# A fused attention and mixture-of-experts block: the last two scatters issued together, and the mixed tiles at other places

## Chip, core and metric

The kernel runs on one core of a Trainium2 chip. The metric is the device time of one execution in microseconds (us); lower is better. The time before is 401.59 us, the median of 3 runs (400.23 to 401.62).

## What is computed

```python
x = x + tanh(g_xattn) * sparse_attention(ctx_512, layernorm(x))   # 4 x 512 x 512
xl = layernorm(x).reshape(2048, 512)                              # 2048 tokens
shared = silu(xl @ shared_gate_w) * (xl @ shared_up_w) @ shared_down_w
top_val, top_idx = top_k(xl @ router_w, 2)                        # 2 of 8 experts
xin = probs.T[:, :, None] * xl[None]                              # probs: sigmoid(top_val), else 0
gate, up = split(einsum('etd,edf->etf', xin, gate_up_w), 2)       # 512 -> 2 x 256
expert_out = einsum('eti,eid->etd', silu(gate) * up, down_w)      # 256 -> 512
return x + tanh(g_ffn) * (shared + expert_out.sum(axis=0))
```

All numbers are float32. Each token goes to two of eight experts, so there are 4096 pairs of token and expert.

## The kernel before

The first half (the attention matrix, the search for its threshold, the two norms, the router) is not touched by the change, and it is not needed to follow it. Its last results are the rows of tokens and the table of pairs, both complete at about 210 us.

**Tiles and jobs.** The pairs are packed into 34 tiles of 128 rows (`MT = 34`). 25 of them are pure: all 128 rows belong to one expert. Nine are mixed (`MIX = 9`): four groups of 32 rows, each group with its own expert. `MIXED` names the places in the order of tiles at which the mixed ones stand. Tiles and the 16 blocks of the shared expert are jobs, `JOBS[0]` to `JOBS[49]`; from tile 7 (job 23) on the job is the tile's number plus 16. Tile 32 is job 48, and tile 33 is the last, job 49.

**One tile.** GpSimd gathers its rows (`gather`), TensorE turns them (`turn_rows`) and multiplies them with the expert's gate and up weights (`up`), ScalarE takes the silu (`silu_of`), VectorE multiplies (`gate`), TensorE turns the result (`turn_h`), ScalarE copies it (`turned_h`), TensorE multiplies it with the down weights (`down`), ScalarE writes the scaled product into a y buffer (`y_of`), and GpSimd adds the rows to the output in DRAM by an indirect DMA (`scatter`). TensorE's order is `up(j)`, `turn_rows`, `down(j-1)`, `turn_h(j)`, `up(j+1)`: one tile lies in the next one's shadow. All orders are written out by hand, engine by engine, and each engine works in order.

**Scatters are chained.** Two tiles can hold the same token, and a scatter that adds reads a row and writes it back. So each scatter waits until the one before has landed:

```python
pool.wait_ge(scattered, 16 * CHAIN.index(t))
```

**Mixed tiles.** For each, VectorE copies four experts' gate and up weights (`stage_up`, four copies of 128x2048) and ScalarE four down weights (`stage_down`) into a staging buffer, which is free when the mixed tile before has used it. A mixed tile can also hold one token twice. So its finished rows in the y buffer go through one more product: `fold` multiplies them with a 128x128 matrix of zeros and ones that adds up the rows of the same token, ScalarE copies the sums back (`folded_y`), and all but one of the twins are sent to a dump row. The matrices are made once by `twin_rows` (TensorE) and `find_twins` (VectorE); `scatter_rows` makes the row numbers. TensorE issues the fold of job j in the middle of `up(j + 2)`:

```python
if c == DC // 2 and folds is not None:
    fold(folds)
```

Before, `MIXED` is 9, 11, 13, ..., 25. So the product in whose middle a fold stands is that of the next mixed tile for eight of nine folds (fold of tile 9 in `up` of tile 11, and so on); only the last, that of tile 25, stands in a pure product.

**y buffers.** `y_slot` gives job j its buffer: two in turn. `Y_FROM = 100` is behind the last job, so the rule for three buffers behind it is never used.

Of the kernel before, what the change touches and what calls it, by code (L numbers as in the profile page):

```python
# [8 lines left out]
I32 = mybir.dt.int32  # L9
# [16 lines left out]
def flamingo_gated_block(nc, x, ctx_in, g_xattn, g_ffn, wq, wk, gamma_raw, router_w, gate_up_w, down_w,  # L26
# [38 lines left out]
    MIXED = (9, 11, 13, 15, 17, 19, 21, 23, 25)  # L65


    CHAIN = (0, 1, 2, 3, 4, 5, 6, 7, 8, 9, 10, 11, 12, 13, 14, 15, 16, 17, 18, 19, 20, 21, 22, 23, 24, 25, 26, 27, 28, 29, 30, 31, 32, 33)

# [14 lines left out]
    Y_FROM = 100  # L84
# [38 lines left out]
    with ExitStack() as stack:  # L123
# [122 lines left out]
        idx_s = tmp[:, 3, 32:32 + MIX].bitcast(I32)  # L246
        etab_u = tmp[0:1, 3, 64:64 + UNITS].bitcast(I32)
# [106 lines left out]
        fold_ps = sem("fold_ps")  # L354
        folded = sem("folded")
# [129 lines left out]
        def _(pool):  # L485
# [64 lines left out]
            def scatter(t):  # L550
# [119 lines left out]
        def _(act):  # L670
# [110 lines left out]
            def y_of(j):  # L781
# [222 lines left out]
            stage_down(2, 0)  # L1004
            stage_down(2, 1)
            folded_y(27)
# [4 lines left out]
            stage_down(2, 2)  # L1011
            stage_down(2, 3)
# [4 lines left out]
            stage_down(3, 0)  # L1017
            stage_down(3, 1)
            folded_y(29)
# [4 lines left out]
            stage_down(3, 2)  # L1024
            stage_down(3, 3)
# [4 lines left out]
            stage_down(4, 0)  # L1030
            stage_down(4, 1)
# [5 lines left out]
            stage_down(4, 2)  # L1037
            stage_down(4, 3)
# [4 lines left out]
            stage_down(5, 0)  # L1043
            stage_down(5, 1)
            folded_y(33)
# [4 lines left out]
            stage_down(5, 2)  # L1050
            stage_down(5, 3)
# [4 lines left out]
            stage_down(6, 0)  # L1056
            stage_down(6, 1)
            folded_y(35)
# [4 lines left out]
            stage_down(6, 2)  # L1063
            stage_down(6, 3)
# [4 lines left out]
            stage_down(7, 0)  # L1069
            stage_down(7, 1)  # L1070
            folded_y(37)
# [4 lines left out]
            stage_down(7, 2)  # L1076
            stage_down(7, 3)
# [4 lines left out]
            stage_down(8, 0)  # L1082
            stage_down(8, 1)
            folded_y(39)
# [4 lines left out]
            stage_down(8, 2)  # L1089
            stage_down(8, 3)  # L1090
# [4 lines left out]
            folded_y(41)  # L1095
# [3 lines left out]
            turned_h(43)  # L1099
            silu_of(44)  # L1100
            turned_rows(29)
            y_of(43)
            turned_h(44)
            silu_of(45)
            turned_rows(30)
            y_of(44)
            turned_h(45)
            silu_of(46)
# [17 lines left out]
        def _(pe):  # L1126
# [120 lines left out]
            def twin_rows(k):  # L1247
# [79 lines left out]
            def down(j):  # L1327
# [16 lines left out]
                for c in range(IC):  # L1344
# [4 lines left out]
                    mm = TE.matmul(y_b[j % 2][:, :], hT[:, j % 2, c], w, start=(c == 0), stop=(c == IC - 1))  # L1349
# [231 lines left out]
            up(29, 27)  # L1581
# [3 lines left out]
            up(30)  # L1585
# [3 lines left out]
            up(31, 29)  # L1589
# [15 lines left out]
            up(35, 33)  # L1605
# [3 lines left out]
            up(36)  # L1609
# [3 lines left out]
            up(37, 35)  # L1613
# [3 lines left out]
            up(38)  # L1617
# [3 lines left out]
            up(39, 37)  # L1621
# [3 lines left out]
            up(40)  # L1625
# [3 lines left out]
            up(41, 39)  # L1629
# [3 lines left out]
            up(42)  # L1633
# [3 lines left out]
            up(43, 41)  # L1637
# [3 lines left out]
            up(44)  # L1641
# [7 lines left out]
            up(46)  # L1649
# [17 lines left out]
        def _(dve):  # L1667
# [311 lines left out]
            def read_plan(g):  # L1979
# [369 lines left out]
```

## Time and profile before

| | |
|---|---|
| median of 3 runs | 401.59 us (400.23 to 401.62) |
| the profiled execution's own time | 399.67 us |
| its span on the core | 397.9 us |
| TensorE busy | 368.6 us, 93% of the span |
| VectorE, ScalarE, GpSimd busy | 228.0, 216.8, 132.8 us |
| mean granted clock of TensorE | 0.981 |

Times in the trace count from the start of the span. A scatter shows twice: as the time that GpSimd takes to write its descriptors, and as a DMA that lands later. Busy shares are means over stages with different limits, so the rows further down are of single stages.

### The profile page before, as it was taken

To read this page: it belongs to the slowest core of one execution; us is meant where nothing else is said; L and a number is where in the kernel's file an instruction comes from. 1 tells how busy PE (TensorE), PEld (TensorE's weight loads), DVE (VectorE), ACT (ScalarE), POOL (GpSimd) and SP (SyncE) were. 2 spreads that over 40 slices of the span, in tenths; PEclk is the share of its full clock that TensorE was granted. 3 is DMA by queue.
4 is the path that set the end of the run, shared out by engine and by line. 5 is a ranking of instruction groups with operands and counts; after the bars stand their busy time and mean duration, and the time that the engine had idled before them with its cause. 6 is when DMAs were issued, how large, how long until landed. Compare 5 with 4: busy or idle time off the path is not lost.

```text
span 397.9 us, 6563 instructions
## 1 busy us (share of the span) xinstructions
PE 368.6 (93%) x2018; PEld 200.8 (50%) x2018; DVE 228.0 (57%) x819; ACT 216.8 (54%) x422; POOL 132.8 (33%) x114
## 2 busy tenths in 40 slices
PE   8859789989999999999999999999999999999950
PEld 4324478467845688558766433433443343444520
DVE  1899999999998689852737635532553350110100
ACT  3594877585762696353222476656665666432320
POOL 2201121110715332222306456543644363444231
PEclk9988999999999999999999999999999999999996
DMA  7999970184767642368323564344534453446442
GB/s 222 384 387 382 389 260 6 21 235 140 218 102 188 162 79 29 53 147 174 41 41 75 87 108 83 79 75 86 83 79 67 95 80 82 69 91 108 53 51 28
DMA packets 29353, 51.12 MB, mean 128 GB/s; under 512 B 4614, under 2 KB 7942, under 8 KB 29318
## 3 DMA queue, kind: packets, MB, share of 16 engines
q0 software_dynamic: 9920, 22.16, 33.3%
q1 hardware_dynamic: 19110, 28.40, 20.3%
q8 instruction: 17, 0.28, 0.3%
q14 instruction: 18, 0.15, 0.1%
q10 hardware_dynamic: 288, 0.13, 0.1%
HBM read 28.60 MB, written 22.09 MB: 127 GB/s over the span
## 4 chain that ended last, share of the span: by engine, by line
PE 65%; DMA 11%; DVE 9%; ACT 8%; issue 4%; SPq 1%; POOLq 0%; POOL 0%; DVEq 0%; ACTq 0%
PE gate_up L1314 14%; PE down L1349 13%; PE gate_up L1299 12%; DMA out_dram<-y_sb,idx 8%; PE gate_up L1308 8%; PE down L1340 4%; PE turned_x L1281 3%; ACT junk L690 3%; PE front L1262 2%; PE turned_h L1324 2%; DMA xs<-in_x_dram 2%; PE front L1173 1%; ACT x L727 1%; DMA out_dram<-y_sb,tmp 1%; ACT sim L685 1%
## 5 line engine op out<-in xcount | busy, mean ns | idle before, releaser
L1314 PE MATMUL gate_up<-w_gu,xT 128*128 x200 | 90.0, 594 | 0.0
L2042 DVE SCALAR_TENSOR_TENSOR h<-gate_up,p_t,silu 128x256 f32<-128x256 f32 x34 | 16.4, 483 | 113.0 <-ACT silu L761 104.0
L566 POOL DMA_INDIRECT out_dram<-y_sb,idx x25 | 42.4, 1697 | 71.5 <-DMA out_dram<-y_sb,idx 33.6
L1299 PE MATMUL gate_up<-xT,w_shgu 128*128 128x128 f32 x512 | 60.0, 276 | 1.1 <-ACT xT L738 1.1
L1299 PEld LDWEIGHTS gate_up<-xT,w_shgu 128*128 128x128 f32 x512 | 58.6, 192 | 3.6 <-issue 2.3
L545 POOL DMA_INDIRECT xg<-x_rows,idx x34 | 45.2, 1329 | 43.5 <-DMA x_rows<-payl 13.5
L790 ACT ACTIVATE y_sb<-down,gates 128x512 f32<-128x512 f32 x50 | 34.2, 687 | 46.0 <-PE down L1349 31.5
L1314 PEld LDWEIGHTS gate_up<-w_gu,xT 128*128 128x128 f32 x200 | 36.3, 190 | 37.3 <-issue 37.3
L1349 PE MATMUL down<-w_dn,hT 128*128 x100 | 47.3, 597 | 0.9 <-ACT hT L770 0.9
L2025 DVE COPY sim<-w_gu 128x2048 f32 x36 | 41.8, 1222 | 0.9 <-DVE oh_e L1990 0.5
L690 ACT ACTIVATE junk<-sim,probe 128x512 int8<-128x512 f32 x44 | 31.2, 712 | 16.6 <-DVE probe L1723 9.7
L761 ACT ACTIVATE silu<-gate_up,p_t 128x256 f32<-128x256 f32 x34 | 16.1, 473 | 44.0 <-PE gate_up L1314 31.7
L801 ACT COPY xs<-w_dn 128x1024 f32 x36 | 36.0, 1046 | 1.2 <-issue 1.1
L1308 PE MATMUL gate_up<-sim,xT 128*32 128x512 f32 x288 | 34.4, 598 | 0.0
L1349 PE MATMUL down<-w_shdn,hT 128*128 128x512 f32 x64 | 30.1, 597 | 0.0
L566 POOL DMA_INDIRECT out_dram<-y_sb,tmp x9 | 15.2, 1687 | 37.9 <-ACT y_sb L805 35.1
L528 POOL DMA_DIRECT2D out_dram<-y_sb x16 | 15.1, 987 | 32.0 <-ACT y_sb L790 32.0
L1281 PEld LDWEIGHTS turned_x<-ident,xg 128*128 128x128 f32 x136 | 15.7, 140 | 19.8 <-issue 19.8
L1349 PEld LDWEIGHTS down<-w_dn,hT 128*128 128x128 f32 x100 | 17.2, 191 | 14.4 <-issue 14.4
L779 ACT COPY xT<-turned_x 128x512 f32<-128x512 f32 x34 | 19.9, 584 | 7.4 <-PE turned_x L1281 6.6
L1281 PE MATMUL turned_x<-ident,xg 128*128 128x128 f32 x136 | 21.1, 278 | 1.2 <-ACT xT L779 0.8
L1324 PEld LDWEIGHTS turned_h<-ident,h 128*128 128x128 f32 x68 | 8.6, 141 | 18.3 <-issue 17.0
(222 smaller groups left out, 503.3 us busy)
## 6 DMA issues: line engine op xcount, KB each, us to landing
w_gu<-in_L_ffn_gate_up_w_dram SPq DMA_DIRECT2D x8, 1024.0 KB
xs<-in_x_dram SPq DMA_DIRECT2D x4, 1024.0 KB, 6.9
w_dn<-in_L_ffn_down_w_dram SPq DMA_DIRECT2D x8, 512.0 KB
out_dram<-xs SPq DMA_DIRECT2D x4, 1024.0 KB, 6.9
x_rows<-x SPq DMA_DIRECT2D x4, 1024.0 KB, 5.0
out_dram<-y_sb POOLq DMA_DIRECT2D x16, 256.0 KB, 4.5
w_gu<-in_ctx_dram SPq DMA_DIRECT2D x4, 256.0 KB, 5.4
xg<-x_rows,idx POOLq DMA_INDIRECT x34, 4.3
```

The lines of the kernel that those rows point to most:

```text
L545: G.indirect_dma_start(out=xg[:, t % XG, :], out_offset=None, in_=x2_rows[0:2 * N, :] if t < EARLY else x2_rows[:, :], in_offset=bass.Indi ...
L566: G.indirect_dma_start(out=out[0:2 * N, :] if t < EARLY else out[:, :], out_offset=bass.IndirectOffsetOnAxis(ap=rows, axis=0), in_=y_at(j) ...
L690: ins = A.activation(junk[:, i - SHARE[b]], sim[:, b, i], ACT.Sign, scale=-1.0, bias=probe[:, k, i:i + 1], accum_out=sgn[:, k, i:i + 1])
L779: A.copy(xT[:, x_slot(j)], x_b[:, :].rearrange("p (c t) -> p c t", c=DC)).then_inc(xt_done, 1)
L790: A.activation(y_at(j), y_b[j % 2][:, :], ACT.Copy, scale=gates[:, 1:2]).then_inc(y_done, 1)
L801: A.copy(unit_dn[:, g], w_dn[:, bass.ds(e * (IC * D), IC * D)]).then_inc(dn_staged, 1)
L1281: mm = TE.transpose(x_b[:, c * P:(c + 1) * P], xg[:, t % XG, c * P:(c + 1) * P], ident[:, :])
L1299: mm = TE.matmul(g_b[j % 2][:, f * P:(f + 1) * P], w_shgu[:, c, f * P:(f + 1) * P], xT[:, x_slot(j), c], start=(c == 0), stop=(c == DC - 1))
L1308: mm = TE.matmul(g_b[j % 2][at, :], xT[:, x_slot(j), c, at], unit_gu[:, r, c * F2:(c + 1) * F2], start=(c == 0), stop=(c == DC - 1))
L1314: mm = TE.matmul(g_b[j % 2][:, :], xT[:, x_slot(j), c], w_gu[:, bass.ds(experts[n] * (DC * F2) + c * F2, F2)], start=(c == 0), stop=(c == ...
L1349: mm = TE.matmul(y_b[j % 2][:, :], hT[:, j % 2, c], w, start=(c == 0), stop=(c == IC - 1))
L2025: V.tensor_copy(unit_gu[:, g], w_gu[:, bass.ds(e * (DC * F2), DC * F2)]).then_inc(gu_staged, 1)
```

## The change

Three things are changed.

1. `PAIR` is tile 32. Its scatter and that of tile 33 need no longer keep apart. Rows of tile 32 whose token tile 33 holds too are sent to the dump row (`idx_p`), and their values, copied by VectorE from the PSUM bank of tile 32's product (`raw_rows`, into `joined`), are added to tile 33's rows by one more matmul in the bank of the last down product. Its 0/1 matrix and the row numbers are made beside those of the mixed tiles. `y_of(48)` waits until `raw_rows` has read the bank. Tile 33's scatter waits for that of tile 31 only.
2. `MIXED` is 9, 12, 15, 18, 20, 22, 24, 26, 28. Staging copies, folds and gates move with it. Five folds now stand in the product of a mixed tile, and four in that of a pure one (tiles 11, 14, 17 and 30).
3. `Y_FROM = 26`: from job 26 on there are three y buffers in turn.

```diff
-    MIXED = (9, 11, 13, 15, 17, 19, 21, 23, 25)
+    MIXED = (9, 12, 15, 18, 20, 22, 24, 26, 28)
...
+    PAIR = MT - 2
...
-    Y_FROM = 100
+    Y_FROM = 26
...
+        row_p = tmp[:, 3, 112:114]
+        twin_p = tmp[:, 3, 114:115]
+        idx_p = tmp[:, 3, 116:117].bitcast(I32)
+        joined = tmp[:, 1, :]
...
+                if t == PAIR:
+                    rows = idx_p
+                    pool.wait_ge(scatter_ready, 1)
...
-                    pool.wait_ge(scattered, 16 * CHAIN.index(t))
+                    pool.wait_ge(scattered, 16 * min(CHAIN.index(t), PAIR))
...
+                if j == job_of("M", PAIR):
+                    act.wait_ge(raw_ready, 1)
                 A.activation(y_at(j), y_b[j % 2][:, :], ACT.Copy, scale=gates[:, 1:2]).then_inc(y_done, 1)
...
+                if k == 2:
+                    mm = TE.matmul(f_b[0][:, P:2 * P], row_p[:, 1:2].to_broadcast([P, P]), ident[:, :], start=True,
+                                   stop=True)
...
-                    mm = TE.matmul(y_b[j % 2][:, :], hT[:, j % 2, c], w, start=(c == 0), stop=(c == IC - 1))
+                    mm = TE.matmul(y_b[j % 2][:, :], hT[:, j % 2, c], w, start=(c == 0),
+                                   stop=(c == IC - 1 and j < NJ - 1))
+                if j == NJ - 1:
+                    pe.wait_ge(raw_ready, 1)
+                    pe.wait_ge(twins_done, 3)
+                    mm = TE.matmul(y_b[j % 2][:, :], fold_m[:, MIX * P:(MIX + 1) * P], joined, start=False, stop=True)
...
+                    V.scalar_tensor_tensor(row_p, f_b[1][:, hi - lo - 2:hi - lo], 1.0, unused[:, hi - lo - 2:hi - lo],
+                                           ALU.subtract, ALU.add)
...
+                if k == 2:
+                    both = fold_m[:, MIX * P:(MIX + 1) * P]
+                    link(V.tensor_scalar(both, f_b[0][:, P:2 * P], row_p[:, 0:1], None, ALU.is_equal))
+                    ins = V.tensor_reduce(twin_p, both, AX_X, ALU.add)
...
+                link(V.tensor_scalar(unused[:, MIX:MIX + 1], row_p[:, 0:1], dump, None, ALU.subtract))
+                link(V.tensor_tensor(unused[:, MIX:MIX + 1], unused[:, MIX:MIX + 1], twin_p, ALU.mult))
+                V.tensor_tensor(idx_p, row_p[:, 0:1], unused[:, MIX:MIX + 1], ALU.subtract).then_inc(scatter_ready, 1)
...
+            def raw_rows():
+                dve.wait_ge(y_ps, job_of("M", PAIR) + 1)
+                V.tensor_copy(joined, y_b[job_of("M", PAIR) % 2][:, :]).then_inc(raw_ready, 1)
```

**TensorE around the first fold.** The rows run from the down product of mixed tile 9 (job 25) to the middle of `up` of tile 11 (job 27). `xs` and `sim` are the staged weights of a mixed tile, `front<-y_sb,x` is the fold. Before:

```order
L1340 MATMUL down<-xs,hT 32x512 [waits dn_staged,y_done,ht_done]
L1340 MATMUL down<-xs,hT 32x512 x7
L1324 MATMUL turned_h<-ident,h 128x128 [waits ht_done,h_ready]
L1324 MATMUL turned_h<-ident,h 128x128
L1308 MATMUL gate_up<-sim,xT 32x512 [waits gu_staged,xt_done,h_ready]
L1308 MATMUL gate_up<-sim,xT 32x512 x7
L1262 MATMUL front<-y_sb,x 128x512 [waits twins_done,y_done]
L1308 MATMUL gate_up<-sim,xT 32x512 x8
```

The same place in the changed kernel:

```order
L1357 MATMUL down<-xs,hT 32x512 [waits dn_staged,y_done,ht_done]
L1357 MATMUL down<-xs,hT 32x512 x7
L1341 MATMUL turned_h<-ident,h 128x128 [waits ht_done,h_ready]
L1341 MATMUL turned_h<-ident,h 128x128
L1331 ISA [waits xt_done,h_ready]
L1331 MATMUL gate_up<-w_gu,xT 128x512
L1331 ISA
L1331 MATMUL gate_up<-w_gu,xT 128x512
L1279 MATMUL front<-y_sb,x 128x512 [waits twins_done,y_done]
L1331 ISA
L1331 MATMUL gate_up<-w_gu,xT 128x512
```

Tile 11 is pure now, so the fold stands between whole matmuls and not between those of 32 columns.

**VectorE behind the ninth twin search.** The rows are the end of `find_twins(2)` and `scatter_rows`; `stage_up(1)`, `weight_of(11)` and `gate(26)` come behind them on the same engine in both kernels. Before:

```order
L2001 TENSOR_SCALAR x<-front,tmp 128x128 [waits twin_ps]
L2002 SCALAR_TENSOR_TENSOR tmp<-front,tmp,upper 128x128
L2008 TENSOR_SCALAR unused<-tmp,cols 128x9 [waits twins_done]
L2009 TENSOR_TENSOR unused<-unused,tmp 128x9 [waits vector_step]
L2010 TENSOR_TENSOR tmp<-tmp,unused 128x9 [waits vector_step]
```

In the changed kernel:

```order
L2025 TENSOR_SCALAR x<-front,tmp 128x128 [waits twin_ps]
L2026 SCALAR_TENSOR_TENSOR tmp<-front,tmp,upper 128x128
L2030 TENSOR_SCALAR x<-front,tmp 128x128
L2031 TENSOR_REDUCE tmp<-x 128x1 [waits vector_step]
L2036 TENSOR_SCALAR unused<-tmp,cols 128x9 [waits twins_done]
L2037 TENSOR_TENSOR unused<-unused,tmp 128x9 [waits vector_step]
L2038 TENSOR_TENSOR tmp<-tmp,unused 128x9 [waits vector_step]
L2039 TENSOR_SCALAR unused<-tmp,cols 128x1
L2040 TENSOR_TENSOR unused<-unused,tmp 128x1 [waits vector_step]
L2041 TENSOR_TENSOR tmp<-tmp,unused 128x1 [waits vector_step]
```

Five instructions are added ahead of `stage_up(1)`: two at 128x128 and three at one column.

**ScalarE at the end.** The rows are `y_of(48)`, `turned_h(49)` and `y_of(49)`. Before:

```order
L790 ACTIVATE y_sb<-down,gates 128x512 [waits scattered,y_ps]
L770 COPY hT<-turned_h 128x256 [waits y_ps,ht_ps]
L790 ACTIVATE y_sb<-down,gates 128x512 [waits scattered,y_ps]
```

In the changed kernel:

```order
L804 ACTIVATE y_sb<-down,gates 128x512 [waits raw_ready,scattered,y_ps]
L782 COPY hT<-turned_h 128x256 [waits y_ps,ht_ps]
L804 ACTIVATE tmp<-down,gates 128x512 [waits scattered,y_ps]
```

The order is the same; the first has one wait more, with the other two queued behind it, and the last writes into the third y buffer.

## Rows read from the trace of the kernel before

**Rows 1.** Windows: busy time and count of each engine, PEclk, DMA share, GB/s.

```profile
200.00:231.00 31.00, 31.00 (x189) 17.28 (x189) 18.56 (x62) 11.67 (x20) 12.23 (x9) 1.00 0.43 68
...
370.00:385.00 15.00, 13.80 (x39) 6.12 (x37) 0.97 (x2) 4.59 (x10) 4.06 (x3) 1.00 0.36 49
```

**Rows 2.** Timeline of GpSimd: scatters of tiles 25, 32 and 33.

```profile
344.70 1.58 POOL L566 DMA_INDIRECT out_dram<-y_sb,tmp  x1 [4.56 <-ACT y_sb L805]
...
384.04 1.55 POOL L566 DMA_INDIRECT out_dram<-y_sb,idx  x1 [3.94 <-DMA out_dram<-y_sb,idx]
...
389.50 1.55 POOL L566 DMA_INDIRECT out_dram<-y_sb,idx  x1 [3.91 <-DMA out_dram<-y_sb,idx]
```

**Rows 3.** The scatters' line L566: time from issue to landing.

```profile
DMA to landing us min/median/max: 4.6/4.9/6.2
```

**Rows 4.** Timeline of ScalarE: folded rows of tile 25, then the end.

```profile
343.35 0.58 ACT L805 COPY y_sb<-front 128x512 f32<-128x512 f32 x1 [1.97 <-PE front L1262]
...
381.64 0.69 ACT L790 ACTIVATE y_sb<-down,gates 128x512 f32<-128x512 f32 x1 [1.24 <-PE down L1349]
382.23 0.36 ACT L770 COPY hT<-turned_h 128x256 f32<-128x256 f32 x1
384.75 0.69 ACT L790 ACTIVATE y_sb<-down,gates 128x512 f32<-128x512 f32 x1 [2.16 <-PE down L1349]
```

**Rows 5.** Timeline of TensorE: up(49), down(48), down(49).

```profile
376.29 3.60 PE L1314 MATMUL gate_up<-w_gu,xT 128*128 x8
379.72 1.88 PE L1349 MATMUL down<-w_dn,hT 128*128 x4
...
382.73 1.98 PE L1349 MATMUL down<-w_dn,hT 128*128 x4 [0.91 <-ACT hT L770]
```

**Rows 6.** Timeline of TensorE: up of tiles 9, 11, 27; L1262 is a fold.

```profile
219.47 3.64 PE L1308 MATMUL gate_up<-sim,xT 128*32 128x512 f32 x32
223.04 0.66 PE L1281 MATMUL turned_x<-ident,xg 128*128 128x128 f32 x4
...
233.23 0.44 PE L1324 MATMUL turned_h<-ident,h 128*128 128x128 f32 x2
233.60 1.92 PE L1308 MATMUL gate_up<-sim,xT 128*32 128x512 f32 x16
235.45 1.13 PE L1262 MATMUL front<-y_sb,x 128*128 128x512 f32 x2
236.51 1.92 PE L1308 MATMUL gate_up<-sim,xT 128*32 128x512 f32 x16
238.36 0.66 PE L1281 MATMUL turned_x<-ident,xg 128*128 128x128 f32 x4
...
340.57 1.88 PE L1314 MATMUL gate_up<-w_gu,xT 128*128 x4
...
344.86 0.60 PE L1281 MATMUL turned_x<-ident,xg 128*128 128x128 f32 x4
```

**Rows 7.** Timeline of VectorE: gate(26), behind stage_up(1).

```profile
232.00 0.48 DVE L2042 SCALAR_TENSOR_TENSOR h<-gate_up,p_t,silu 128x256 f32<-128x256 f32 x1
```

**Rows 8.** VectorE groups by line and shape: count, busy us, mean ns.

```profile
L2025 DVE COPY sim<-w_gu 128x2048 f32 x36 | 41.8, 1222 | 0.9 <-DVE oh_e L1990 0.5 <-issue 0.3
...
L1823 DVE SCALAR_TENSOR_TENSOR xs<-front,c,xs 128x512 f32<-128x512 f32 x16 | 11.8, 746 | 1.8 <-PE front L1173 1.2 <-PE front L1176 0.5
...
L2002 DVE SCALAR_TENSOR_TENSOR tmp<-front,tmp,upper 128x128 f32<-128x128 f32 x9 | 3.1, 346 | 0.0
...
L1924 DVE COPY tab_f<-front 128x128 f32<-128x128 f32 x1 | 0.3, 283 | 0.0
...
L2008 DVE TENSOR_SCALAR unused<-tmp,cols 128x9 f32<-128x9 f32 x1 | 0.3, 296 | 0.0
```

**Rows 9.** Windows near the start, as in rows 1.

```profile
16.00:20.00 4.00, 2.17 (x6) 0.62 (x4) 3.27 (x14) 2.60 (x7) 0.63 (x1) 1.00 1.05 386
20.00:24.00 4.00, 3.04 (x4) 1.31 (x5) 3.79 (x15) 4.00 (x11) 0.00 (x0) 0.67 1.05 387
```

More of the change, by code:

```diff
@@ L64, in flamingo_gated_block @@
     assert (2 * T - E) // UNIT + E - 4 * FULL <= UNITS
-    MIXED = (9, 11, 13, 15, 17, 19, 21, 23, 25)
+    MIXED = (9, 12, 15, 18, 20, 22, 24, 26, 28)
     CHAIN = (0, 1, 2, 3, 4, 5, 6, 7, 8, 9, 10, 11, 12, 13, 14, 15, 16, 17, 18, 19, 20, 21, 22, 23, 24, 25, 26, 27, 28, 29, 30, 31, 32, 33)
+    PAIR = MT - 2
+    assert PAIR not in MIXED and PAIR + 1 not in MIXED
     def column_of(t):
@@ L1010, in _ @@
             turned_h(29)
-            stage_down(2, 2)
-            stage_down(2, 3)
+            stage_down(2, 0)
+            stage_down(2, 1)
+            folded_y(28)
             silu_of(30)
@@ L1049, in _ @@
             turned_h(35)
-            stage_down(5, 2)
-            stage_down(5, 3)
+            stage_down(4, 0)
+            stage_down(4, 1)
+            folded_y(34)
             silu_of(36)
@@ L1062, in _ @@
             turned_h(37)
-            stage_down(6, 2)
-            stage_down(6, 3)
+            stage_down(5, 0)
+            stage_down(5, 1)
+            folded_y(36)
             silu_of(38)
@@ L1075, in _ @@
             turned_h(39)
-            stage_down(7, 2)
-            stage_down(7, 3)
+            stage_down(6, 0)
+            stage_down(6, 1)
+            folded_y(38)
             silu_of(40)
@@ L1088, in _ @@
             turned_h(41)
-            stage_down(8, 2)
-            stage_down(8, 3)
+            stage_down(7, 0)
+            stage_down(7, 1)
+            folded_y(40)
             silu_of(42)
@@ L1099, in _ @@
             turned_h(43)
+            stage_down(8, 0)
+            stage_down(8, 1)
+            folded_y(42)
             silu_of(44)
@@ L1103, in _ @@
             turned_h(44)
+            stage_down(8, 2)
+            stage_down(8, 3)
             silu_of(45)
@@ L1107, in _ @@
             turned_h(45)
+            folded_y(44)
             silu_of(46)
@@ L2251, in _ @@
             gate(27)
+            weight_of(13)
+            gate(28)
             stage_up(2, 0)
@@ L2255, in _ @@
             stage_up(2, 3)
-            weight_of(13)
-            gate(28)
             weight_of(14)
             gate(29)
+            weight_of(15)
+            gate(30)
+            weight_of(16)
+            gate(31)
             stage_up(3, 0)
@@ L2263, in _ @@
             stage_up(3, 3)
-            weight_of(15)
-            gate(30)
-            weight_of(16)
-            gate(31)
+            weight_of(17)
+            gate(32)
+            weight_of(18)
+            gate(33)
+            weight_of(19)
+            gate(34)
             stage_up(4, 0)
@@ L2271, in _ @@
             stage_up(4, 3)
-            weight_of(17)
-            gate(32)
-            weight_of(18)
-            gate(33)
+            weight_of(20)
+            gate(35)
+            weight_of(21)
+            gate(36)
             stage_up(5, 0)
@@ L2279, in _ @@
             stage_up(5, 3)
-            weight_of(19)
-            gate(34)
-            weight_of(20)
-            gate(35)
+            weight_of(22)
+            gate(37)
+            weight_of(23)
+            gate(38)
             stage_up(6, 0)
@@ L2287, in _ @@
             stage_up(6, 3)
-            weight_of(21)
-            gate(36)
-            weight_of(22)
-            gate(37)
+            weight_of(24)
+            gate(39)
+            weight_of(25)
+            gate(40)
             stage_up(7, 0)
@@ L2295, in _ @@
             stage_up(7, 3)
-            weight_of(23)
-            gate(38)
-            weight_of(24)
-            gate(39)
+            weight_of(26)
+            gate(41)
+            weight_of(27)
+            gate(42)
             stage_up(8, 0)
@@ L2303, in _ @@
             stage_up(8, 3)
-            weight_of(25)
-            gate(40)
-            weight_of(26)
-            gate(41)
-            weight_of(27)
-            gate(42)
             weight_of(28)
```

71 lines of the change are left out of this document (31 added, 40 removed).

## The prediction

> **What bounds the kernel now.** I read the windows first, since the page's 93% for TensorE is a mean over stages. Behind 200 us TensorE is without a gap: 31.00 us busy of 31.00 in the first stretch, and none of the stretches up to 370 shows one; from 370 to 385 it is busy 13.80 of 15.00, always at the full granted clock [rows 1]. So up to the down product of tile 32 every microsecond of TensorE counts. Then I read GpSimd's timeline, because the span ends 8.4 us behind its last instruction: the last scatter is issued at 389.50, and what held it was a DMA, the scatter before [rows 2]. Its own data had long been there: ScalarE wrote tile 33's rows from 384.75 to 385.44 [rows 4]. The chain takes (384.04 - 344.70) / 7 = 5.62 us a scatter between tiles 25 and 32, and the last step takes 5.46 [rows 2], of which some 4.9 are the flight [rows 3]. So two things in a row set the end: TensorE up to about tile 25, whose fold comes late, and then nine chained scatters, the last of which starts 389.50 - 385.44 = 4.06 us behind its rows.
>
> **Step 1, the last scatter.** It no longer waits for tile 32's. It can start when its rows are there, plus what GpSimd needs from rows to issue where nothing else holds it: 344.70 - (343.35 + 0.58) = 0.77 us [rows 2, 4]. With the rows at 385.44 that would be 386.21, a gain of 3.29. But the change makes the rows later (step 2).
>
> GpSimd must also have issued tile 32's scatter, and that one stays chained. The last fold, now that of tile 28, stands in `up(46)`. A pure tile takes TensorE (376.29 - 340.57 - 0.86) / 6 = 5.81 us (`up(43)` to `up(49)` with one fold between them, whose 0.86 is worked out in step 3) [rows 5, 6]. So `up(46)` starts at 376.29 - 3 x 5.81 = 358.9 today, with nine folds behind it. In the changed kernel eight are behind it and the ninth is in it: start near 357.8 (with the 0.17 of the sum below), half a product of 1.72 (half of 379.72 - 376.29 = 3.43 [rows 5]) and the fold end near 360.4, and the scatter of tile 28 starts near 360.4 + 0.6 + 0.77 = 361.8. Four steps of 5.62 later tile 32's starts at 384.3, and with 1.55 for its descriptors [rows 2] GpSimd is free at 385.8. So the chain gains nothing from the new places, and it is not in the way either if tile 33's rows come behind 385.1.
>
> **Step 2, what is put ahead of tile 33's rows.** ScalarE works in order: `y_of(48)`, `turned_h(49)`, `y_of(49)` stand behind each other. `y_of(48)` starts at 381.64, `turned_h(49)` at 382.23, and TensorE, idle for 0.91 us, starts the last down product at 382.73 when that copy is there [rows 4, 5]. Now `y_of(48)` waits for VectorE's copy of the 128x512 bank. So the whole copy goes into the path, as TensorE has nothing else left. The trace has no such copy. The nearest rows: the same size out of PSUM with a second operand takes 746 ns (L1823); at 128x128 the two-operand form takes 346 (L2002) and the copy 283 (L1924), 63 less [rows 8]. 746 - 63 = 0.68, and with a hand-off of 0.05 it is 0.73. Bounds: 0.51 (283 ns plus 384 columns at the 0.60 ns a column of the staging copy, L2025) and 0.80.
>
> By the Trainium skill ("VectorE: DVE Perf Modes", section "Why PSUM operands drop a tier") a PSUM operand caps a float32 copy at one element a cycle, where one from SBUF can do two. Taken alone the staging copy's rate would make this term 0.17 less; the rule speaks for the longer figure, which the PSUM rows give too.
>
> One matmul is added in the last bank: float32, 128x128 by 128x512, the same form as a fold. In a pure product a fold costs (344.86 - 340.57) - 3.43 = 0.86 us [rows 5, 6]. It is last, so it counts whole: 0.86. Step 2 costs 0.73 + 0.86 = 1.59 us.
>
> **Step 3, the folds' places.** A mixed `up` alone takes 223.04 - 219.47 = 3.57 us; with a fold in its middle 238.36 - 233.60 = 4.76, so a fold costs 1.19 there and 0.86 in a pure product [rows 6]. Three folds move from mixed to pure products: 3 x 0.33 = 0.99 us less on a TensorE that has no gap, so it arrives whole at job 48. Everything else of a mixed tile costs the same in its new place. Staging keeps its distance: each `stage_up` stands behind the gate of the mixed tile before, and the next gate needed is one pure `up` later, as today; in the three wide spacings the deadline for the weights even moves out by a tile. I cost it at nothing; if the cover were missing, the price is a copy of 1.22 us [rows 8].
>
> **Step 4, the longer twin search.** One more 128x128 turn on TensorE: a product of 128 columns is a quarter of the 0.86, 0.22 us. Behind it VectorE has five more instructions ahead of `stage_up(1)`: the comparison 0.35 + 0.04 for the hand-off, the sum over 128 columns about 0.33, and three small ones, of which the first is like L2008 with 0.30 and the others about half of it: 0.64 in all. With the 0.22 that it waits for TensorE VectorE is late by 1.6 (1.2 to 1.9). Behind the four staging copies stands `gate(26)`, which ends at 232.00 + 0.48 = 232.48 [rows 7]; TensorE turns its result at 233.23 [rows 6]. The slack is 0.75, and 0.97 with TensorE's own 0.22. So a stall of about 0.6 us (0.2 to 0.9) is new at `turn_h(26)`, and on a gapless TensorE it stays to the end. GpSimd's chain has room there, and the gather behind `weight_of(11)` is three tiles ahead of its use.
>
> **Step 5, three y buffers.** No row of the timeline shows `y_of` held by a scatter in the tail; TensorE has no gap, so two buffers cost nothing. I cost the third at nothing.
>
> **Sum.** To job 48: - 0.99 + 0.22 + 0.6 = - 0.17. Tile 33's rows are written from 384.75 - 0.17 + 1.59 = 386.17 to 386.86, its scatter starts at 387.63 instead of 389.50: - 1.9 us. Both have the same flight and the same 3.7 us or so behind the landing. The profiled execution's 399.67 would become 397.8. It lies 1.9 us under the median of the runs shown, to which the same difference applies: 401.59 - 1.9 = 399.7. Without stall and with the short copy it is - 2.8 us, with the stall at 0.9, a copy of 0.80 and 0.5 us of other frictions - 1.0. The four executions known spread over 1.95 us, and the median is at their upper edge, so the low end goes to 397.8.
>
> **Rivals.**
> - *The overlap is paid in flight* (0.08). Tile 33's scatter is issued while tile 32's is in the air, 3.5 us behind it. Flights range from 4.6 to 6.2 [rows 3]; at the upper end the last lands 1.3 us later: - 0.6 us, 401.0. Against it: the first has landed when the second's data begin to move, and gathers overlap scatters all through the tail while the chain keeps 5.6 a step.
> - *The join doesn't free the scatter* (0.05): GpSimd or its queue keeps the second back until the first lands, near 389.0. - 0.5 us, 401.1. Nothing in the trace shows two scatters out at once, so it can't be excluded.
> - *The clock falls in the last wait* (0.06), the case on the other side. TensorE will be idle for 0.91 + 0.73 = 1.6 us ahead of its last six matmul instructions. Near the start a stretch with 2.17 us busy of 4 is followed by one at 0.67 of the clock [rows 9]. At the lower of its two levels, 1.2 instead of 2.4 GHz, the six instructions take 0.86 us each instead of 0.43, 2.6 more in all. Then it is - 1.9 + 2.6 = + 0.7, 402.3. It decides if the fall comes before the last product is under way. Against it: the wait of 0.91 brought none, and the fall near the start shows only in the next window.
> - *Late h elsewhere* (0.07): VectorE's or ScalarE's queue is late at each of the moved staging places and not at one. Each tenth of a microsecond at nine places is 0.9; from 0.2 a place on the gain is gone: 401.5 and more.
> - *The flight is short.* The Trainium skill ("DMA: Bandwidth & Descriptors", section "Anatomy of one DMA — SWDGE (gpsimd) path") fits such a transfer as 2.0 us plus bytes over 436 GB/s, 2.6 us for 256 KB. The chain's step would then be some 3.4 us and shorter than a tile, no scatter would wait for the one before, and the change would only add step 2's 1.59 less 0.17. The time by that would be 403.0. All 34 flights took 4.6 us or more [rows 3], so it has 0.01.
>
> **How the numbers follow.** The forecast has the remaining 0.73. What can be told from no change is 0.5%, 2.0 us, and - 1.9 lies just under it. So the forecast's 0.73 falls on both sides, with more on the fast one, since the median known of before sits at the upper edge of its executions: 0.44 faster by over 0.5%, and nothing of the rivals; 0.48 is within (0.29 of the forecast, the two rivals at - 0.5 and - 0.6, and half of the two on the slow side); 0.08 is slower, part of it the runs' own scatter. The range 397.8 to 401.5 leaves out the slow rivals and little else.
>
> **What the changed profile would show.** Right: the last scatter released by ScalarE and not by a DMA, about 0.8 us behind the rows, with two scatters 3.5 us apart; a VectorE copy of about 0.68 us between `down(48)` and `y_of(48)`; TensorE idle about 1.6 us ahead of the last product, which is 0.86 longer; four folds at 0.86; a gap of about 0.6 us at `turn_h(26)`. Wrong: a gap in TensorE at a staging place, a lower granted clock from 382 us on, or a last flight of over 5 us.

## The result, and the profile after

| | before | after |
|---|---|---|
| median | 400.56 us (20 runs, 399.00 to 401.62) | 397.81 us (20 runs, 396.75 to 399.17) |
| the profiled execution's own time | 399.67 us | 397.96 us |
| its span on the core | 397.9 us | 396.2 us |

The ratio of the medians is 0.9931, with a 95% interval of 0.9920 to 0.9942: the change takes 2.75 us off (2.3 to 3.2). That is faster by 0.69%.

The page of the changed kernel: the span, the busy time of each engine, the granted clock in 40 slices, and the shares of the chain that ended last.

```profile
span 396.2 us, 6577 instructions
PE 368.9 (93%) x2020; PEld 202.3 (51%) x2022; DVE 230.2 (58%) x826; ACT 216.9 (55%) x422; POOL 132.9 (34%) x114
...
PEclk9986999999999999999999999999999999999997
...
PE 70%; DVE 12%; DMA 7%; ACT 4%; issue 3%; POOL 1%; SPq 1%; POOLq 0%; DVEq 0%; ACTq 0%
```

No engine's total shows the gain. It shows in the timeline of GpSimd; these are the scatters of tiles 28, 31, 32 and 33, which answer to [rows 2]:

```profile
362.37 1.58 POOL L578 DMA_INDIRECT out_dram<-y_sb,tmp  x1 [3.94 <-ACT y_sb L819]
...
379.05 1.55 POOL L578 DMA_INDIRECT out_dram<-y_sb,idx  x1 [4.07 <-DMA out_dram<-tmp,idx]
384.69 1.55 POOL L578 DMA_INDIRECT out_dram<-y_sb,tmp  x1 [4.08 <-DMA out_dram<-y_sb,idx]
387.61 1.55 POOL L578 DMA_INDIRECT out_dram<-tmp,idx  x1 [1.38 <-ACT tmp L804]
```

What stands behind the arrow has changed in the last row: ScalarE's rows release the last scatter, no longer a DMA. It starts 2.92 us behind the scatter of tile 32, where a step of the chain takes (384.69 - 362.37) / 4 = 5.58.

The timeline of TensorE, VectorE and ScalarE at the end, to be held beside [rows 4, 5]:

```profile
379.96 1.88 PE L1366 MATMUL down<-w_dn,hT 128*128 x4
...
381.88 0.69 DVE L2045 COPY tmp<-down 128x512 f32<-128x512 f32 x1 [0.72 <-PE down L1366]
382.68 0.69 ACT L804 ACTIVATE y_sb<-down,gates 128x512 f32<-128x512 f32 x1 [2.05 <-DVE tmp L2045]
383.27 0.36 ACT L782 COPY hT<-turned_h 128x256 f32<-128x256 f32 x1
383.77 1.98 PE L1366 MATMUL down<-w_dn,hT 128*128 x4 [1.72 <-ACT hT L782]
...
385.59 1.02 PE L1371 MATMUL down<-tmp,x 128*128 128x512 f32 x2
386.65 0.69 ACT L804 ACTIVATE tmp<-down,gates 128x512 f32<-128x512 f32 x1 [3.02 <-PE down L1371]
```

TensorE's last wait grew from 0.91 to 1.72 us, since the copy (L2045) stands ahead of `y_of(48)`, and `turned_h(49)`, which releases TensorE, stands behind that. The joined matmul (L1371) stands ahead of the last rows. These end at 386.65 + 0.69 = 387.34, and the scatter starts at 387.61, only 0.27 behind them.

Windows of the changed kernel, columns as in [rows 1]:

```profile
200.00:231.00 31.00, 31.00 (x192) 17.62 (x191) 18.11 (x67) 10.90 (x20) 11.79 (x9) 1.00 0.44 70
231.00:260.00 29.00, 28.59 (x134) 12.27 (x133) 10.46 (x24) 16.76 (x27) 13.91 (x9) 1.00 0.46 84
370.00:385.00 15.00, 13.29 (x39) 6.26 (x38) 1.66 (x3) 4.34 (x9) 3.41 (x3) 1.00 0.40 51
```

One stretch in the middle has lost 0.41 us of TensorE: 28.59 of 29. The granted clock is 1.00, the upper of the two levels, through the last wait too. The gap is at `turn_h(26)`. The timeline of VectorE and TensorE shows it behind the longer twin search (L2030, L2031 are new) and the staging copies (L2060), where `gate(26)` (L2077) comes late:

```profile
226.93 0.35 DVE L2030 TENSOR_SCALAR x<-front,tmp 128x128 f32<-128x128 f32 x1
227.31 0.29 DVE L2031 TENSOR_REDUCE tmp<-x 128x1 f32<-128x128 f32 x1
...
229.26 4.64 DVE L2060 COPY sim<-w_gu 128x2048 f32 x4 [0.34 <-issue]
...
233.91 0.48 DVE L2077 SCALAR_TENSOR_TENSOR h<-gate_up,p_t,silu 128x256 f32<-128x256 f32 x1
...
234.44 0.44 PE L1341 MATMUL turned_h<-ident,h 128*128 128x128 f32 x2 [0.41 <-DVE h L2077]
```

**A common mark.** The first half, which nothing here changes, takes some tenths more or less in each execution. So I count from the last one-column matmul of the row numbers (`128*1` in the timeline), which is among the last work of that half on TensorE: it starts at 209.49 in the profile before and at 209.91 in the one after. From this mark on, in us:

| kernel | ratio to before (95%) | last rows start | last scatter starts | end of span |
|---|---|---|---|---|
| before | | 175.26 | 180.01 | 188.4 |
| after | 0.9931 (0.9920 to 0.9942) | 176.74 | 177.70 | 186.3 |
| e1 join only | 0.9947 (0.9927 to 0.9968) | 177.71 | 178.68 | 187.1 |
| e2 places only | 0.9974 (0.9960 to 0.9988) | 174.26 | 179.48 | 188.0 |
| e3 third buffer only | 0.9999 (0.9980 to 1.0019) | 175.26 | 180.62 | 189.1 |
| e4 h first | 0.9913 (0.9891 to 0.9934) | 175.57 | 176.53 | 185.0 |
| e5 before again | one execution | 175.27 | 179.93 | 188.3 |
| e6 chained again | 0.9997 (0.9974 to 1.0019) | 176.74 | 179.99 | 188.5 |
| e7 search later | 0.9937 (0.9914 to 0.9959) | 175.05 | 176.21 | 185.2 |
| e8 two buffers | 0.9940 (0.9917 to 0.9963) | 176.74 | 177.70 | 186.2 |
| e9 waits behind | one execution | 176.73 | 177.69 | 186.4 |
| e10 folded last | 1.0007 (0.9995 to 1.0018) | 175.27 | 179.95 | 188.5 |
| e11 before, a third time | one execution | 175.92 | 182.17 | 190.6 |
| e12 all three | 0.9903 (0.9881 to 0.9924) | 175.05 | 176.01 | 184.9 |

The work up to the last rows repeats within a hundredth or two (before, e3, e5 and e10; after, e6, e8 and e9), except in e11. There the last rows waited for the scatter of tile 31, which still held their y buffer (0.66 us late), because the chain of that execution ran late. So a tenth can be read there from one profile, which the whole time doesn't allow.

### The profile page after: what moved, and what is told of

Its sections match the earlier page's. It is cut to its first block, busy times and chain, and to the rows that moved or that the text cites. A ratio compares the mean times of both kernels' runs of the same rounds, so it can differ in the third digit from the quotient of the medians.

```text
span 396.2 us, 6577 instructions
## 1 busy us (share of the span) xinstructions
PE 368.9 (93%) x2020; PEld 202.3 (51%) x2022; DVE 230.2 (58%) x826; ACT 216.9 (55%) x422; POOL 132.9 (34%) x114
## 4 chain that ended last, share of the span: by engine, by line
PE 70%; DVE 12%; DMA 7%; ACT 4%; issue 3%; POOL 1%; SPq 1%; POOLq 0%; DVEq 0%; ACTq 0%
PE gate_up L1331 16%; PE down L1366 14%; PE gate_up L1316 12%; PE gate_up L1325 8%; PE down L1357 4%; PE turned_x L1298 3%; DMA out_dram<-y_sb,idx 2%; PE front L1279 2%; PE turned_h L1341 2%; DVE ge_words L1754 2%; DMA xs<-in_x_dram 2%; PE down L1149 2%; PE front L1187 1%; ACT junk L702 1%; DVE ge_words L1773 1%
## 5 line engine op out<-in xcount | busy, mean ns | idle before, releaser
L2077 DVE SCALAR_TENSOR_TENSOR h<-gate_up,p_t,silu 128x256 f32<-128x256 f32 x34 | 16.4, 483 | 111.7 <-ACT silu L773 97.3
L578 POOL DMA_INDIRECT out_dram<-y_sb,idx x20 | 35.8, 1792 | 55.6 <-ACT y_sb L804 16.4
L804 ACT ACTIVATE y_sb<-down,gates 128x512 f32<-128x512 f32 x42 | 28.7, 687 | 36.0 <-PE down L1366 24.9
L2060 DVE COPY sim<-w_gu 128x2048 f32 x36 | 41.9, 1223 | 1.0 <-DVE oh_e L2014 0.5
L578 POOL DMA_INDIRECT out_dram<-y_sb,tmp x6 | 9.5, 1575 | 25.2 <-ACT y_sb L819 21.2
```

The lines of the kernel that those rows point to most:

```text
L578: G.indirect_dma_start(out=out[0:2 * N, :] if t < EARLY else out[:, :], out_offset=bass.IndirectOffsetOnAxis(ap=rows, axis=0), in_=y_at(j) ...
L2060: V.tensor_copy(unit_gu[:, g], w_gu[:, bass.ds(e * (DC * F2), DC * F2)]).then_inc(gu_staged, 1)
```

## Experiments

### e1 to e3: one part of the change each

e1 is the kernel before with the joined last scatter alone, e2 with the new places of the mixed tiles (and the orders of all engines that go with them), e3 with the third buffer. The core of e1, e2 and e3:

```diff
-                    pool.wait_ge(scattered, 16 * CHAIN.index(t))
+                    pool.wait_ge(scattered, 16 * min(CHAIN.index(t), PAIR))
```

```diff
-    MIXED = (9, 11, 13, 15, 17, 19, 21, 23, 25)
+    MIXED = (9, 12, 15, 18, 20, 22, 24, 26, 28)
```

```diff
-    Y_FROM = 100
+    Y_FROM = 26
```

> The kernel before with the join alone: tile 32's rows joined in the last bank, its scatter and the last one together, the longer twin search. Mixed tiles stay at 9, 11, ..., 25 and two y buffers. Theory A (the terms add up): against the kernel before TensorE loses 0.22 and a stall of 0.4 at turn_h(26), the last rows come another 1.66 later, at 384.75 + 2.3 = 387.0 to 387.7, and the last scatter is issued 0.3 to 0.8 behind: 388.0 to 388.5 instead of 389.5. That is 1.0 to 1.5 us faster than before (ratio 0.9963 to 0.9975). Theory B (the join holds the whole gain, the places nothing): 2.7 us faster, ratio 0.9932. The last scatter waits for ScalarE in both.

> The kernel before with the mixed tiles at 9, 12, 15, 18, 20, 22, 24, 26, 28 and nothing else. Theory A: TensorE gains 3 x 0.33 = 1.0 us, no gap is new. The last fold (tile 28) ends near 359.6, its scatter is issued near 361.0 instead of 361.8, and five chained scatters follow it at 5.6 each, so the end comes 0.7 us earlier (0.4 to 1.0), ratio 0.9975 to 0.999. The last scatter still waits for the one before. Theory B: no difference, since the chain of scatters sets the end. Theory C (the missing 0.8 us of the forecast lies in the places): 1.3 us or more faster.

> The kernel before with three y buffers from job 26 on and nothing else. Theory A: nothing, ratio 0.999 to 1.001, since no row of the kernel before shows ScalarE held by a scatter behind job 26. Theory C (the third buffer frees ScalarE in a way that the trace puts down to another releaser): 0.3 us or more faster, with less idle time ahead of y_of.

e1 gives 0.9947, 2.1 us off; e2 0.9974, 1.0 us off; e3 0.9999, nothing. The sum is 3.1 us, where the whole change has 2.75, within the intervals. e1's ratio lies between its two theories, and its interval reaches into both; at the mark its last scatter is 180.01 - 178.68 = 1.33 us earlier, which is theory A's 1.0 to 1.5. The marks give each term's size. e2's last rows come 175.26 - 174.26 = 1.00 us earlier: the three folds that left mixed products. e1's last rows come 2.45 later: copy, matmul and the late `h`. e3's come at 175.26, as before: the third buffer moves nothing.

In e2 the last scatter is still released by the one before, and yet its start is 180.01 - 179.48 = 0.53 earlier from the mark. The chain starts earlier there. GpSimd's row of tile 28, the last folded one, in e2:

```profile
361.99 1.58 POOL L566 DMA_INDIRECT out_dram<-y_sb,tmp  x1 [4.02 <-ACT y_sb L805]
```

Its folded rows release it and no DMA, 361.99 - 210.34 = 151.65 from the mark. In the kernel before the same tile's scatter starts at 361.76, 152.27 from the mark. The 0.62 in between passes down five chained steps nearly whole, as theory A had it (0.7, from 0.4 to 1.0). So the places do move the end: through the last fold that the chain waits for.

### e4: h ahead of the last tile but one

The kernel after, with two calls on ScalarE exchanged. Theory: the copy of the bank is in the path only because `y_of(48)`, which has to wait for it, stands ahead of `turned_h(49)`, which TensorE waits for. Rival: the copy would only come back elsewhere.

```diff
             silu_of(49)
-            y_of(48)
             turned_h(49)
+            y_of(48)
             y_of(49)
```

> The changed kernel with ScalarE's last three in another order: turned_h(49), y_of(48), y_of(49). The copy of tile 32's bank by VectorE then lies beside turned_h(49) and the last product. Theory A (the copy is in the path because y_of(48) stands ahead of turned_h(49)): TensorE's last wait falls from 1.7 to about 0.5 us, the last rows come 1.1 us earlier, the last scatter at 386.5 where GpSimd is just free (384.7 + 1.55 + 0.2): 1.0 us faster than the changed kernel, 3.7 faster than before, ratio 0.9905. Rival: the matmul of the join waits for the copy anyway, so nothing is won, ratio 0.993.

The ratio is 0.9913, 3.5 us under the 400.53 measured beside it. ScalarE, TensorE and GpSimd in the timeline of e4:

```profile
382.22 0.37 ACT L782 COPY hT<-turned_h 128x256 f32<-128x256 f32 x1 [1.46 <-PE turned_h L1341]
...
382.73 1.98 PE L1366 MATMUL down<-w_dn,hT 128*128 x4 [0.55 <-ACT hT L782]
...
386.57 1.55 POOL L578 DMA_INDIRECT out_dram<-tmp,idx  x1 [0.63 <-ACT tmp L804]
```

TensorE's wait is 0.55 instead of 1.72, and the last scatter starts 177.70 - 176.53 = 1.17 us earlier from the mark. So the copy was in the path by the order of two lines alone, and with it the 0.36 that the wait had before the change. The medians of after and e4 differ by 0.75 us and the intervals of the two ratios overlap, so the shift is shown by the mark and not by them.

### e5, e6 and e8: the kernel before again, the chain put back, two buffers

e5 is the kernel before without an edit, profiled a second time to see how its chain varies. e6 is the kernel after with the last wait put back: all costs of the join are there, and the overlap isn't. e8 is the kernel after with two buffers.

```diff
-                    pool.wait_ge(scattered, 16 * min(CHAIN.index(t), PAIR))
+                    pool.wait_ge(scattered, 16 * CHAIN.index(t))
```

```diff
-    Y_FROM = 26
+    Y_FROM = 100
```

> The kernel before, unedited, for a second profile. Theory D (the profile on which the forecast rests showed a lucky execution): from the end of the plan's products (the last one-row matmul, 209.49 in the first profile) to the last scatter's issue it was 180.0 us, with 5.60 a step in the chain between tiles 25 and 33; here it is 180.4 to 180.8, with steps of 5.65 to 5.70, as in the kernel with three buffers only, 180.6 and 5.68. Rival: again 180.0 and 5.60, and the missing 0.6 us lies in something the change does.

> The changed kernel with the wait put back: tile 33's scatter again waits until that of tile 32 has landed; copy, matmul and search stay. Theory A (the freed wait is the whole gain at the end, and it is worth the last step less what the join puts ahead of the rows): the last scatter at 384.7 + 4.9 + 0.7 = 390.3 instead of 387.6, 2.7 us slower than the changed kernel and level with the kernel before less what the places give there: ratio to before 0.998 to 1.0. Rival (the gain comes from the places): under 1 us slower than the changed kernel, ratio 0.994.

> The changed kernel with two y buffers instead of three. Theory A: the third buffer is worth nothing here either, the ratio to before stays at 0.993 (0.992 to 0.994), and no row of ScalarE shows y_of waiting for a scatter in the tail. Theory C (the third buffer is needed once the mixed tiles stand later, as a folded tile keeps its buffer longest): 0.3 us or more slower than the changed kernel, with y_of held by a DMA behind 340 us.

e6 is back at the kernel before: 0.9997. GpSimd's last row there, and ScalarE's:

```profile
389.76 1.55 POOL L578 DMA_INDIRECT out_dram<-tmp,idx  x1 [3.82 <-DMA out_dram<-y_sb,tmp]
```

```profile
386.51 0.69 ACT L804 ACTIVATE tmp<-down,gates 128x512 f32<-128x512 f32 x1 [3.02 <-PE down L1371]
```

The rows are as in the kernel after, 176.74 from the mark, and the last scatter starts 389.76 - 387.20 = 2.56 us behind them, held by the one before. So without the freed wait nothing is left of the gain. e6 has the new places too. In e2 they start the chain 0.62 us earlier; in e6 the scatter of tile 28 starts at 362.22, 152.45 from the mark, no earlier than before. The longer search makes the difference: it keeps TensorE 0.79 later from `turn_h(26)` on (see the steps below), and the fold of tile 28 with it. So in e6 places and search cancel, and the freed wait makes the gain. The intervals of e2, 0.9974 (0.9960 to 0.9988), and e6 overlap, so this rests on the marks.

e8 has 0.9940 and rows and scatter at the same marks as after: the third buffer costs and gives nothing in the executions profiled. (With two buffers a late chain can hold the last rows, as e11 shows; what the third would give there was not measured.) e5 has the last scatter where the kernel before has it, 179.93 from the mark against 180.01, so its rival held and theory D didn't.

### e7: the pair's search behind gate(26)

e4, with the two 128-column steps and the three small ones moved behind `gate(26)`, so that `stage_up(1)` is no longer late. Theory: the gap of 0.41 at `turn_h(26)` goes, and the end comes earlier by as much. Rival: with the two scatters closer together the overlap is paid in flight.

```diff
             gate(26)
+            pair_search()
             weight_of(12)
```

> The kernel with h first at the end, and with VectorE's five instructions for the pair behind gate(26) instead of ahead of the staging of the second mixed tile. Theory A (the search makes TensorE wait at turn_h(26), and on an engine without gaps that stays to the end): that gap of 0.4 us is gone, the last rows come 0.4 us earlier than with h first alone, and the last scatter follows them until GpSimd's descriptors for tile 32's scatter bound it: 0.2 to 0.4 us faster than with h first alone, ratio to before 0.9903. Rival: the gap opens again at the next staging place or is swallowed by the chain, no difference, 0.9913.

TensorE's timeline of e7 at `turn_h(26)`, now without a wait:

```profile
234.72 0.44 PE L1341 MATMUL turned_h<-ident,h 128*128 128x128 f32 x2
```

GpSimd's last two rows in e7:

```profile
385.04 1.55 POOL L578 DMA_INDIRECT out_dram<-y_sb,tmp  x1 [4.00 <-DMA out_dram<-y_sb,idx]
386.89 1.55 POOL L578 DMA_INDIRECT out_dram<-tmp,idx  x1 [0.30 <-issue]
```

The scatters' line in that window, from issue to landing of the two:

```profile
DMA to landing us min/median/max: 4.9/5.1/5.3
```

The gap is gone and the last rows come 0.52 earlier from the mark (175.05 for 175.57). The end doesn't follow: 185.2 for e4's 185.0, ratio 0.9937, where 0.9903 was expected. Two things hold it. GpSimd is busy with tile 32's descriptors to 386.59 and issues 0.30 behind them, so the rows, there at 386.42, wait for it, and the last scatter starts only 0.32 earlier. And the last flight takes 5.3 us, where it took 4.8 in e4. That is what the rival says, on one execution.

### e9 to e12: the hand-off, a third profile of before, all together

The open question was why the last scatter started 0.27 us behind its rows, where [rows 2, 4] have 0.77 for a folded tile. Theory: a folded tile has two more waits (for the fold and for the row numbers), and what stands behind the wait that comes last costs time. e9 gives tile 33's scatter two such waits, both long satisfied; e10 is the kernel before with the wait for the fold as the last one ahead of the scatter; e12 is e7 with e10's edit. Rival: the hand-off differs for another reason. e11 is the kernel before without an edit.

```diff
+                if t == PAIR + 1:
+                    pool.wait_ge(folded, MIX)
+                    pool.wait_ge(scatter_ready, 1)
```

```diff
                 if m is not None:
-                    pool.wait_ge(folded, m + 1)
                     pool.wait_ge(scatter_ready, 1)
...
+                if m is not None:
+                    pool.wait_ge(folded, m + 1)
                 G.indirect_dma_start(out=out[0:2 * N, :] if t < EARLY else out[:, :],
```

> The changed kernel with two waits more for the last scatter, both long satisfied, behind the wait for its rows. They name the search's and the folds' semaphores, as a mixed tile's scatter does. Theory E (waits that stand behind the one that holds are worked off after it, at some 0.25 us each): from the rows' end to the issue 0.77 us instead of 0.27, as for the folded tiles. Rival F (a folded tile's scatter is issued later for another reason, such as its row numbers): 0.27 as in the changed kernel.

> The kernel before with the order of GpSimd's waits changed for a mixed tile: those that are long satisfied first, that for the folded rows last. Theory E: from folded rows to issue 0.27 us instead of 0.77, so tile 25's scatter and the eight chained behind it start 0.5 us earlier, 0.5 us faster than before (ratio 0.9988), which is at the edge of what the runs can tell; the trace tells it. Rival F: 0.77 stays, no difference.

> The kernel before, unedited, for a third profile. The first two run from the plan's last product to the span's end in 188.4 and 188.3 us, the changed kernel and the one with two buffers in 186.3 and 186.2, which is 2.1 us less, where the medians differ by 2.75 (2.3 to 3.2). Theory D (the chained end varies between executions and the two profiles lie low): 188.7 to 189.1, as the kernel with the third buffer only. Rival: 188.3 again, and the medians' rest stays open.

> The changed kernel with h first at the end, the search for the pair behind gate(26), and the folded wait last. Theory E: the scatters of tiles 28 to 32 start 0.5 us earlier than with the first two alone, so that GpSimd is free before the last rows are written; the last scatter is issued 0.27 us behind them and 2.2 us behind the one before, where its flight was 4.8 and not the 5.3 of 1.85 us: from the plan's last product to the end 184.5 to 184.8 us instead of 185.2, and 3.6 to 3.9 us faster than before, ratio 0.9905. Rival: the last flight stays at 5.3 us, 185.1 us.

**Hand-off.** In e9 the last scatter still starts 0.27 behind its rows (387.44 to 387.71), in e10 that of tile 25 still 0.80 behind (344.24 to 345.04). So neither the two satisfied waits behind the one that holds nor moving the wait for the fold to the end changes it by more than 0.03: the theory fell. What remains is a figure by kind of release: 0.27 to 0.28 behind `y_of` in after, e1, e4, e8, e9 and e12, and 0.76 to 0.81 behind `folded_y` in every kernel. Why is not settled. A folded tile takes its row numbers from another table, but the scatter of tile 32 in the kernel after does so too, and its chained step is 5.64 us beside 5.61 and 5.67 for its neighbours. Two differences were never separated: a copy releases where an activation does, and the wait for `y_done` stands first in `scatter` in every kernel here, while that for the fold always stands behind it.

**The chain.** e11, the same program as before, ends at 190.6 from the mark and not at 188.4; the expected 188.7 to 189.1 missed it too. GpSimd's timeline of e11, tiles 27 and 28:

```profile
355.93 1.60 POOL L566 DMA_INDIRECT out_dram<-y_sb,idx  x1 [3.24 <-issue]
...
363.23 1.58 POOL L566 DMA_INDIRECT out_dram<-y_sb,idx  x1 [4.39 <-DVE p_junk L2032]
...
391.19 1.55 POOL L566 DMA_INDIRECT out_dram<-y_sb,idx  x1 [4.04 <-DMA out_dram<-y_sb,idx]
```

From the scatter at 355.93 to the next there are 7.30 us, where the profile before has 5.67. This is the line's answer for that one scatter:

```profile
DMA to landing us min/median/max: 6.5/6.5/6.5
```

In the profile before the same scatter took 4.9. The name behind the arrow at 363.23 is a VectorE instruction that had long been done; the wait that ended last is the flight. The 1.6 us stay to the end, since no later step has room to make them up; the other 0.5 lie in steps of 0.1 to 0.2. The kernel after has room: behind tile 32's descriptors GpSimd would be free to issue at 384.69 + 1.55 + 0.30 = 386.54, and the last scatter starts 1.07 us later than that. By this estimate a chain that is late by less doesn't move the last issue. It brings the two scatters closer, though, down to 1.85 us, where e7's last flight took 5.3.

**All three.** e12 has 0.9903, the lowest median of all, 396.59 us; its interval takes in e4's 0.9913, and the end from the mark, 184.9, lies between its two theories. GpSimd's end in e12:

```profile
383.59 1.55 POOL L579 DMA_INDIRECT out_dram<-y_sb,tmp  x1 [4.03 <-DMA out_dram<-y_sb,idx]
385.57 1.55 POOL L579 DMA_INDIRECT out_dram<-tmp,idx  x1 [0.43 <-ACT tmp L805]
```

The last scatter's flight in e12:

```profile
DMA to landing us min/median/max: 5.2/5.2/5.2
```

The last scatter starts 0.52 us earlier from the mark than in e4, and the span ends at 184.9 for 185.0: the flight again takes nearly all of it. e10's own effect on time is nil (1.0007).

## Why the prediction was wrong in size and right in mechanism

The direction and the mechanism held, and the time lies at the low edge of the range (397.81, edge 397.8). But - 1.9 us was forecast and - 2.75 came, and the chances put "within 0.5%" first, where the measurement says faster. Of the 1.9 us between the forecast 399.7 and 397.81 the change explains 0.85; the other 1.03 is the base, since three runs of before gave a median of 401.59 and twenty give 400.56. That the time still touched the range is luck in this respect. Step by step, with the marks:

| step | forecast | measured |
|---|---|---|
| 1: scatter released by its rows | yes | yes, and e6, without that, is back at 0.9997 |
| 1: from rows to issue | 0.77 | 0.27 |
| 2: copy and hand-off in ScalarE's order | 0.73 | 0.80 (`turned_h(49)` 1.04 later, of which 0.24 is the shift of `down(48)`) |
| 2: joined matmul | 0.86 | 0.86 (last product to rows 2.88, before 2.02) |
| 3: three folds moved | - 0.99 | - 1.00 (e2) |
| 4: twin matmul and stall | 0.22 + 0.6 = 0.82 | 0.30 + 0.49 = 0.79 |
| 5: third buffer | 0 | 0 (e3, e8) |
| 1: tile 32's scatter, still chained | 384.3 | 384.69, of which 0.42 is the later mark |
| last rows, in all | + 1.42 | + 1.48 |
| last scatter | - 1.87 | - 2.31 |

The parts of step 4 are read from the mark: TensorE starts `up(26)` at 228.13 for 227.41 before, 0.30 later, and `turn_h(26)` at 234.44 for 233.23, 0.79 later. The idle time of 0.41 in the row is a little less than the stall's 0.49. e1 gives the same 0.79: 2.45, less the 0.80 and 0.86 of the two rows above. One bound of the recorded sum is off: without stall and with the short copy its own terms make - 1.87 - 0.6 - 0.22 = - 2.7, and not - 2.8.

**The step that failed** is in step 1: "what GpSimd needs from rows to issue where nothing else holds it: 344.70 - (343.35 + 0.58) = 0.77 us". I took it from the scatter of a folded tile, since in the tail of before no other one is released by its rows. The last tile is a pure one, and there the same hand-off measured 0.27 to 0.28, in six kernels. With it the sum would have been - 2.4 us, 0.6%, and so beyond the 0.5% below which the forecast told no change. That term is 0.50 of the missing 0.85; the rest is the base below. The right row was in the profile before, outside the tail. The first of the two is in ScalarE's timeline, the second in GpSimd's:

```profile
225.45 0.69 ACT L790 ACTIVATE y_sb<-down,gates 128x512 f32<-128x512 f32 x1 [1.13 <-PE down L1349]
```

```profile
226.42 2.25 POOL L566 DMA_INDIRECT out_dram<-y_sb,idx  x1 [3.03 <-ACT y_sb L790]
```

A pure tile's rows end at 226.14 and release the scatter at 226.42: 0.28, for the same two lines that meet at the end.

**The base.** From the mark the profiled executions give - 2.1 us at the end, the medians - 2.75. I said that the same difference applies to both. It need not: before ends with a chain that takes every late flight into the end, and after has 1.07 us of room for one. The five profiles with before's chain and rows (before, e3, e5, e10, e11) end at 188.3 to 190.6 from the mark, with a mean of 189.0; the three of after's (after, e8, e9) at 186.2 to 186.4, with a mean of 186.3. The difference, 2.7, is that of the medians. But 0.4 of it hangs on one execution, e11, and the 20 runs of before spread hardly wider than those of after (2.6 us against 2.4). So a chain that often runs later than the one I read would explain the rest, but it is not shown, and the 0.35 us stay open. e1 and e2 have the same open rest: their profiles gain 1.33 and 0.53 at the last scatter, their medians 2.1 and 1.0.

**The rivals.** The clock didn't fall in a wait of 1.72 us: 1.00 in the stretch around it. GpSimd did issue a second adding scatter with the first in the air, so the join did free it. A late `h` came at one place and not at nine. The overlap was hardly paid in flight by this change: at 2.92 us between the two, the last flight is 4.9, where the chained last one of before took 4.7. It is 4.7 at 3.15 (e8), 5.0 at 2.76 (e9), 4.7 at 2.73 (e1) and 4.8 at 2.18 (e4), then 5.2 at 1.98 (e12) and 5.3 at 1.85 (e7). With the two closer the rival seems right; each figure is one execution. The fifth, a flight of 2.6 us, is what the Trainium skill ("DMA: Bandwidth & Descriptors", section "Anatomy of one DMA — SWDGE (gpsimd) path") gives by its fit; the traces disagree, with 4.6 us or more for the last flight in every kernel here.

**The copy.** 0.69 us for 128x512 out of PSUM and 0.283 for 128x128 [rows 8] make (0.69 - 0.283) / 384 = 1.06 ns a column, where the staging copy within SBUF has 0.60. The Trainium skill ("VectorE: DVE Perf Modes", section "Why PSUM operands drop a tier") says that a PSUM operand costs a float32 copy its faster mode; the trace agrees.

## What to carry to other kernels

A chain of transfers that wait for each other sets the end even where the engines are full up to it; letting the last link go pays as long as the work put in its place is shorter than the wait, here 1.66 us for a wait of 4.06. When a wait is given to an instruction early in an engine's order, look at what is queued behind it: exchanging two calls took the copy out of the path. And take a hand-off from a row with the same releaser and the same wait, because here two on one engine differed by 0.5 us for the same scatter instruction.

## What the runs showed of the hardware

- GpSimd starts a scatter 0.27 to 0.28 us behind the activation that releases it, and 0.76 to 0.81 behind the copy of a folded tile; two satisfied waits more leave the first figure unchanged (e9), and with the wait for the fold put last the second is 0.80 for 0.77 (e10).
- Two adding scatters of 256 KB can be in the air at once. The second's flight is 4.7 to 5.0 us when it starts 2.18 us or more behind the first (five kernels), and 5.2 and 5.3 at 1.98 and 1.85 (one execution each).
- The same scatter of the same program, that of tile 27 in the kernel before, took 4.9 us in two executions and 6.5 in a third (e11).
- TensorE's granted clock stayed at 1.00 through a wait of 1.72 us in the kernel after.
- A fold between whole matmuls costs TensorE 237.32 - 236.46 = 0.86 us, the figure that the prediction had worked out, now read at the tile that it speaks of:

```profile
234.71 1.92 PE L1331 MATMUL gate_up<-w_gu,xT 128*128 x4
236.46 1.02 PE L1279 MATMUL front<-y_sb,x 128*128 128x512 f32 x2
237.32 1.88 PE L1331 MATMUL gate_up<-w_gu,xT 128*128 x4
```
